# A Mamba-like two-layer network on one core: the hand-laid tables of interleavings are replaced

## The chip, the cores and the metric

The kernel runs on one core of one Trainium2 chip, in a single launch. The metric is device microseconds of that core, the median of three runs. The core has TensorE (PE in the profile, its weight loads PEld), VectorE (DVE), ScalarE (ACT), GpSimd (POOL) and SyncE (SP), which issues all DMAs of this kernel.

## The reference: what is computed

Eight samples go one after the other through two layers. Layer 0 is an input projection of 192 channels to 2 x 384, a depthwise 3x3 convolution, a state-space scan with two orders of the 64x64 image (12 heads of 64 channels, 32 states), a gate, an output projection and an MLP. Layer 1 has a branch of three dense convolutions and a branch with layernorm, projection, depthwise convolution and a selective scan in four directions over 192 channels with 16 states each:

```
def step(h, t):
    u_t, d_t, b_t, c_t = t
    h = jnp.exp(d_t[..., None] * A) * h + (d_t * u_t)[..., None] * b_t[:, :, None, :]
    return (h, jnp.einsum('bkdn,bkn->bkd', h, c_t))
```

The four directions are summed, normed, gated, projected, and joined with the convolution branch.

## The kernel before

**Slots.** The selective scan of layer 1 is the backbone. For one sample it is 384 units (4 directions x 4 column blocks x 24 groups of 8 channels x 16 states, a tile of 128 x 1024). A unit is handled in a slot. In slot u, ScalarE makes the decay `dA` of unit u+1 (exp, line 1202) from a 512 KB DMA `dA<-dld`; TensorE expands the input of unit u+1 into `PU` (2 matmuls, waits for scan u-1) and sums the product of unit u-3 into `PY` (4 matmuls); VectorE multiplies `PU` by B (line 1588) and runs the scan `H` (line 1820); GpSimd multiplies `H` by C into `HC` (line 1984). The scans are the same for every sample and follow one another without a break.

**Rounds.** Everything else is laid between the slots as steps. Round r (r = 1 to 8) holds the 384 scan slots of sample r-1, phases a to f of sample r, which prepare the next sample's scan, and, from round 2 on, the closing phases g and h of sample r-2. Round 0 has no scan. Round 1 is of kind "first", rounds 2 to 7 are "middle", round 8 is "last".

**Phases.** a: projection and depthwise convolution of layer 0 (`a.conv`), then tokens written to DRAM (`tkd`). b: the state-space part of layer 0 in chunks, 8 set-up steps (`b.setup`) and 64 units, each with `b.fetch` (SP loads `TK` from `tkd`), `b.prepare` (TensorE, ScalarE, GpSimd), `b.mix` (GpSimd, line 1917), `b.out` (TensorE, VectorE) and `b.store`. c: gate, output projection and MLP, 8 strips. d: three convolutions. e: layernorm, projection, depthwise convolution. f: the inputs of the scan (`f.steps`, `f.split`). g and h: sum of directions, norm, gate, output.

**What sets the order.** Each engine has its own table: for every third of a slot (`p` = 0, 1, 2) a digit says how many steps of the list are placed ahead of it. A step that has nothing to do on an engine costs nothing there. Where a middle round also holds phases g and h, a second table `AMID` says how their steps go between those of a to f. No scheduler acts at run time: each engine takes its instructions in the order written and waits on semaphores. The steps of a phase stand in the same order on every engine before and after; only where they fall among the slots differs.

```
    for slot, n in zip(slots, TAKEN.get((kind, engine), [0] * len(slots))):
        out += itertools.islice(left, n)
        out.append(slot)
    return out + list(left)
```

Of the kernel before, what the change touches and what calls it, by code (L numbers as in the profile page):

```python
# [174 lines left out]
def counts(text):  # L175
    out, n = [], 0
    for c in text:
        n += DIGITS.index(c)
        if c != "Z":
            out.append(n)  # L180
            n = 0
    return out
# [4 lines left out]
        "a0009000000003003002007400000002402000000000000000000000000000000000j00006000600000600000000006000000006000006"  # L187
        "00000000T00100100w00100010w00100100w00100100w00100100w00100010w00100100900000600100100100000000000500020100000"
        "40040040000050090050034020050045000050090053040034020050090077007050030013020050090050043020050090053061013020"
        "05007003402005007003402005004302005009005205003402005009503402000500304207005304003402005009007700705003001302"  # L190
        "00500900500330200400500000000000000000800010000300000330000000400100c00500000000400100100100200000400200500100"
        "00030020010020010000040020050010000050000010020010000040020050010000030030000020010001030020050010000030020010"
        "0200100000400300300100200100100100100000300300210000000200010200100000300000100000000000000000000b003003004003"
        "00300200400300500300300400300300300400300300300400300500300300400300300300400300300500300300400300300400400300"
        "30040030030050030030030040030030020000000050020020030010050030030020010000000000060020040040010020030040020010"
        "0400100200300200590000700800500900900900900900900900d00900900900500000000000000000000000b100002002004300004007"
        "4000020032030002007000002003030020020032020000023002"),
    ("first", "ACT"): counts(
        "c0000001000009000000a00000001000700000008003001000004000300000001000500000000001b00001001004001001000004600000"
        "00200220000100300Qx00001001000x0000100l000d0000l00000cx00001001000x00001001000e0000100000110000000200230000000"  # L200
        "0000900000004002c00002005007200007005002c00002005007700002007007j00002000005700002007007700005002007c020000050"
        "07200005007007200005007007200005007002c00002005007700002007007c00000002007c00002005007700002007007j00002000005"
        "700002007007700004002003006000000002002002000000000005000003200004000003e0000000000400000000400100000200400150"
        "00040000000000040010005000010010050040000000005000000000025000000050040000000000041000000020041000050040000000"
        "00004001000002004001400000003000300000000002300000000002400000002002100000000000000000006000100001001000100001"
        "001000m00000000000a0000000000b00000000b00000000b000000b00000000000b0000000000b00000000b00000000b000000b0000000"
        "0000b0000000000b00000000b00100000000c0002000000010024000010050033000030030011000000020035000010010044000000040"
        "01600001000007a00008009009900000009009i0000000100hi0000000100h00000000a001000000000001501001000002600003004003"
        "3000020030032000030050012000000080008000000010028000"),
    ("first", "DVE"): counts(  # L210
        "0e09000000007000003000000008600000200000000007001000000000000300000000000000000000O000000000000000000000000000"
        "00000000000Q00000000y00000000y00000000y00000000y00000000y00000000y00000000600000000000000900000201000202000000"
        "000000000a0070030430400340030430040070030430430400340030430430430430470030040070030430430040030430430430430040"
        "03043040034003043040034003043004007003043043040034003043043043004007003043043043040034003043043043043047003004"
        "00700304304003300303401000200000000000003102100003000000300102100004001b00500000000401000100200100002003002000"
        "00500100300100100210000200300200500000130100100000200100200300200000500100320000000200100200300200000500100300"
        "10010020010020030020000040030000010002000000000000009000002000000000000007000000010000020000000000000000000000"
        "00000000000000000000000000000000000000000000000000000000000000000000000000000000000000000000000000000000000000"
        "00000000000000000000000000000000000000000ZZZ200100200200300300300300300300000000000500200500500500000500000500"
        "000500000000000000900000680090000900900900900900900900900900900900900900300000000000000000000000000000000i00a0"  # L220
        "0300000600300700300000000600300700300000000000600300700"),
    ("first", "POOL"): counts(
        "000g0000040060000000090000080000000070040000040010000000000010000000000000000000000000000000000000000000000000"
        "0000000000Zy00000000y00000000y00000000y00000000y00000000y00000000y00000000000000000000000000000m00000000000000"
        "a00000700700000700700700000700700700000700700700700000700700700e0070000070070000070070070000070070070070070000"
        "0700700700000700700700000700700700000700700700700000700700700700700000700700700700700000700700700e007000007007"
        "00000700700600000600400000300000000000000200000000900000000000000b00000000000h00000000000000000000000000000000"
        "l00000000000000000000000000000000l00000000000000000000000000000000l00000000000000000000000000000000l0000000000"
        "0000000000000000000000000000000000000000000000000000000000000000000000000000000000000K000000000000000000000000"
        "00000000000000000000000000000000000000000000000000000000000000000000000000000000000000000000000000000000000000"  # L230
        "000000000000000000000000000000000000000ZZZ30000000000000000000000000000000000000000000000000000000000000000000"
        "0000000000000000000000Ze00800i00900000900r00000000900r00000000900900000000b00000000000000000000000000000000v00"
        "200000400300300400300200400000300300200200300400200300000"),
    ("first", "SP"): counts(
        "0000c000000006004000003600000004002000006002006000004004000002000000003000006006000006000000000006000006000000"
        "00600000000400R000002v0000200000x00100100w00100100w000002v0000200000x00100100d00100100100100000000400000400900"
        "00000060000000070070070070000070070000070070070070070000070070070077007000070000070070070070000070070070070070"
        "00007007007000007007007000007007000007007007007007000007007007007000007007007007007007000007007007007700700007"
        "00000700700100600000600700200000000000000000800000000000000000a00000000000g00000000000000000000000f00000600000"
        "000000000000000000000f00000600000000000000000000000000f00000600000000000000000000000000f0000060000000000000000"  # L240
        "0000000000f00000000000000000000000000000g000000000000000000b00000000000000000000007002001001000001001001000002"
        "00000000000000000000000000G00000000000000000000m00000000000000000m00000000000000000000m00000000000000000m00000"
        "000000000000m00000000000c00000000000c00500000000200300300300300300000000000000000000000c0000050000050000050000"
        "0500500000000500040000000000000000000000000000000000000000000000000000000ZZn0000000000000011000060020003000000"
        "0b00230000400600000300300300000a0000000060000030000064"),
    ("middle", "PE"): counts(
        "0t00000000400300300000200000300400200400200200000000000000000000000000000000g300006000000006000000006000006000"
        "000600600000T00100100w00100100w00100001w0010010000w00100100w00100100w00100100900000060000200000100000000000500"
        "02010000040040040050034020050030060052070053040020050070034020050070034020050043020050090052050034020050090077"
        "00705003001302005009007700705003001302005009005003402005009005003006005207005304003402005009007700705003001302"  # L250
# [2223 lines left out]
```

How the kernel before makes its waits and increments, by code:

```python
    def take_over(self, e, phase):  # L553
        for name, n in ENDS[phase]:
            e.wait_ge(*self.at(name, n, phase))
        for name in END_DMAS[phase]:
            of = (SHARED[name] if name in SHARED else DMAS[name])[phase]
            e.wait_ge(*self.at(name, of, phase))
# [269 lines left out]
def begin(e, X):  # L829
    if X.n == 0:
        e.wait_ge(X.K.S["b_dve"], SETUP["b_dve"])
    else:
        X.K.samples[X.n - 1].take_over(e, "f")
# [9 lines left out]
    def bank(step, j=0):  # L844
        held = X.before(step, j)
        if held:
            pe.wait_ge(*held)
        return X.bank(step, j)
# [4 lines left out]
    def a_turn(i, p):  # L854
        if p:
            return
        if X.n == 0 and i == 0:
            pe.wait_ge(S["b_dve"], SETUP["b_dve"])
        pe.wait_ge(*X.at(f"xin{i % 2}", 16 * (i // 2 + 1), "a"))
        for hh in range(2):
            pb = bank(("a.turn", i, 0), hh)
            for q in range(4):
                t = pe.transpose(pb[0:96, q * 128:(q + 1) * 128], K.XI[:, i % 2, q, hh * 96:(hh + 1) * 96], K.IDENT)
            t.then_inc(S["a_turn"], 1)
# [1 line left out]
    def a_project(i, j):  # L866
        if i == 0 and j == 0:
            pe.wait_ge(*X.at("weights", 32, "a"))
        pe.wait_ge(*X.at("a_xT", 2 * i + 2))
        pb = bank(("a.project", i, j))
        for k in range(2):
            t = mm(pb[:, :], K.wx[:, k, j * 128:(j + 1) * 128], K.XT[:, i % 2, k, :], k == 0, k == 1)
        t.then_inc(S["a_proj"], 1)
# [126 lines left out]
    def c_outp(i, m):  # L1000
        pe.wait_ge(*X.at("c_yr", 2 * (3 * i + 2) + 2))
        pb = bank(("c.outp", i, m))
```

## Time and profile before

| | us |
|---|---|
| median of 3 runs (18377.16 to 18397.39) | 18393.42 |
| the profiled execution, its own time | 18391.18 |
| its span, first to last instruction | 18389.4 |
| rounds 2 to 7 (13207.0), mean of one | 2201.2 |
| mean granted TensorE clock | 0.82 |

The profile gives busy time of an engine as a union of its instructions. In a stretch where two engines are busy for nearly all of it, both limit it; where none is, instructions wait for one another or for DMAs. A granted clock of 1.00 is 2.4 GHz, 0.50 is 1.2 GHz, and a value between is a mean over the stretch. Round r's scans stand in the trace at rows 384(r-1) to 384r of line 1820, so a slot has a time: round 4 runs from 7846.9 to 10051.4 us, and its slots 60, 79, 156, 162, 240, 250, 266, 305, 320 and 362 begin at 8232.2, 8337.3, 8827.6, 8861.2, 9230.8, 9270.6, 9377.4, 9578.7, 9658.8 and 9872.9 us. In phase b, slots 88, 100, 120 and 132 begin at 8387.0, 8452.1, 8590.9 and 8667.2 us. Round 1 runs from 1373.3 to 3437.8 us.

### The profile page before, as it was taken

To read this page: it belongs to the slowest core of one execution; us is meant where nothing else is said; L and a number is where in the kernel's file an instruction comes from. 1 tells how busy PE (TensorE), PEld (TensorE's weight loads), DVE (VectorE), ACT (ScalarE), POOL (GpSimd) and SP (SyncE) were. 2 spreads that over 40 slices of the span, in tenths; PEclk is the share of its full clock that TensorE was granted. 3 is DMA by queue.
4 is the path that set the end of the run, shared out by engine and by line. 5 is a ranking of instruction groups with operands and counts; after the bars stand their busy time and mean duration, and the time that the engine had idled before them with its cause. 6 is when DMAs were issued, how large, how long until landed. Compare 5 with 4: busy or idle time off the path is not lost. (4 is left out here: it accounts for less than half of the span.)

```text
span 18389.4 us, 229305 instructions
## 1 busy us (share of the span) xinstructions
PE 14799.7 (80%) x75328; PEld 6584.1 (36%) x75328; DVE 14337.4 (78%) x10683; ACT 9054.4 (49%) x15627; POOL 10798.0 (59%) x5940
## 2 busy tenths in 40 slices
PE   7877889788887888878888788878889788885655
PEld 5423533244332443235332353324523244331202
DVE  3237689877887788877888768887789777889997
ACT  3245445654456444664447544465445644455332
POOL 3225756756557665666557565575655766557563
PEclk8988898788888888887988889778798888886555
DMA  2226576756766578665786657765686666868775
GB/s 91 83 80 188 161 195 174 206 161 179 195 173 202 160 190 196 170 196 157 194 197 185 175 159 203 188 198 162 170 201 175 203 164 180 195 174 216 183 189 141
DMA packets 1564886, 3223.74 MB, mean 175 GB/s; under 512 B 296592, under 2 KB 730064, under 8 KB 1562192
## 3 DMA queue, kind: packets, MB, share of 16 engines
q1 hardware_dynamic: 1563728, 3209.07, 65.2%
q8 instruction: 632, 10.35, 0.3%
q14 instruction: 526, 4.31, 0.1%
HBM read 2474.94 MB, written 733.48 MB: 174 GB/s over the span
## 5 line engine op out<-in xcount | busy, mean ns | idle before, releaser
L1984 POOL TENSOR_TENSOR HC<-H,BR 128x1024 f32<-128x1024 f32 x3072 | 7357.2, 2399 | 4784.3 <-DVE H L1820 3268.2
L1820 DVE TENSOR_TENSOR_SCAN H<-dA,CR,PU 128x1024 f32<-128x1024 f32 x2304 | 5397.6, 2343 | 393.5 <-ACT CR L1202 212.6
L1202 ACT ACTIVATE dA<-dA,A 128x1024 f32<-128x1024 f32 x3072 | 3502.7, 1142 | 1607.4 <-DMA dA<-dld 1557.8
L1588 DVE TENSOR_TENSOR PU<-PU,BR 128x1024 f32<-128x1024 f32 x3072 | 3725.5, 1213 | 379.2 <-PE PU L852 345.9
L852 PE MATMUL PU<-PT,SELB 96*128 96x512 bf16 x6144 | 2282.1, 460 | 2022.8 <-DVE H L1820 1880.1
L852 PE MATMUL PB<-RA,RB 128*128 128x64 f32 (+3 forms) x10992 | 3128.6, 438 | 73.5 <-DVE RA L1591 68.0
L852 PE MATMUL PY<-HC,CB 128*32 128x256 f32 x24576 | 2409.4, 471 | 119.0 <-POOL HC L1984 108.5
L852 PEld LDWEIGHTS PB<-RA,RB 128*128 128x128 f32 (+2 forms) x10992 | 1745.1, 205 | 1357.8 <-issue 1240.5
L852 PE MATMUL PB<-RA 128*32 128x64 f32 (+2 forms) x11712 | 1723.2, 325 | 456.3 <-DMA RA<-tkd 392.9
L852 PEld LDWEIGHTS PU<-PT,SELB 96*128 96x128 bf16 x6144 | 545.4, 106 | 3685.4 <-issue 3484.8
L1820 DVE TENSOR_TENSOR_SCAN H<-dA,PU 128x1024 f32<-128x1024 f32 x768 | 1752.1, 2281 | 134.2 <-POOL HC L1984 70.4
L1917 POOL TENSOR_TENSOR RB<-RA,RB 128x768 f32<-128x768 f32 x512 | 930.4, 1817 | 1157.2 <-issue 647.4
L852 PEld LDWEIGHTS PB<-RA 128*32 128x32 f32 (+2 forms) x11712 | 1035.8, 164 | 1215.3 <-issue 564.9
L1202 ACT ACTIVATE RA<-PB 32x128 f32<-32x128 f32 (+3 forms) x2776 | 1078.4, 389 | 653.1 <-PE PB L852 608.3
L852 PE MATMUL PB<-RA,PX 96*128 96x512 f32 x2304 | 1131.8, 631 | 108.4 <-ACT RA L1202 95.1
L1202 ACT ACTIVATE YS<-PY 128x256 f32<-128x256 f32 x768 | 292.3, 381 | 1846.7 <-PE PY L852 1846.5
L852 PEld LDWEIGHTS PY<-HC,CB 128*32 128x32 f32 x24576 | 530.3, 119 | 1797.8 <-issue 1531.5
L1202 ACT ACTIVATE RB<-PB 128x128 f32<-128x128 f32 (+4 forms) x1344 | 364.5, 313 | 1442.7 <-PE PB L938 918.3
L1588 DVE TENSOR_TENSOR RA<-RA,PB 128x384 f32<-128x384 f32 x512 | 281.9, 551 | 944.4 <-PE PB L852 942.4
L1202 ACT ACTIVATE CR<-H 128x1 f32<-128x1 f32 x3072 | 590.9, 192 | 854.8 <-DVE H L1820 851.9
L852 PE MATMUL PB<-XT,RB 96*128 96x512 f32 x1536 | 794.9, 657 | 76.8 <-DMA XT<-xTd 39.7
L852 PE MATMUL PB<-RB 96*128 96x128 bf16 (+1 forms) x4608 | 640.4, 263 | 113.5 <-ACT RA L1202 94.7
(180 smaller groups left out, 17582.9 us busy)
## 6 DMA issues: line engine op xcount, KB each, us to landing
dA<-dld SPq DMA_DIRECT2D x3072, 512.0 KB, 6.0
PT<-ptd SPq DMA_DIRECT2D x2304, 64.0 KB, 4.3
BR<-bcd SPq DMA_DIRECT2D x256, 512.0 KB, 7.6
ptd<-RA SPq DMA_DIRECT2D x176, 576.0 KB, 5.8
y0d<-RA SPq DMA_DIRECT2D x512, 192.0 KB, 9.6
RA<-y0d SPq DMA_DIRECT2D x128, 768.0 KB, 6.7
yd<-YS SPq DMA_DIRECT2D x768, 128.0 KB, 5.0
tkd<-RB SPq DMA_DIRECT2D x256, 262.0 KB, 3.8
```

The source lines that it names most:

```text
L852: return nc.tensor.matmul(out, w, x, start=start, stop=stop, skip_group_check=True)
L1202: return ac.activation(out, in_, f, **kw)
L1588: return v.tensor_tensor(out, a, b, op)
L1820: v.tensor_tensor_scan(h, a, x, 0.0 if first else K.CR[:, gi:gi + 1], MUL, ADD).then_inc(S["s_scan"], 1)
L1917: po.tensor_tensor(K.MM[u % 2].rearrange("p (h t) -> p h t", h=6), K.EE[u % 2].rearrange("p (h t) -> p h t", h=6), K.GS[u % 2].unsqueeze(1 ...
L1984: po.tensor_tensor(K.HC[:, w % NHC, :], K.H[:, w % NH, :], K.BR[:, (w // 24) % NBR, 1, :], MUL).then_inc(S["s_mulC"], 1)
```

## The change

Only numbers in the tables `TAKEN` (all three kinds) and `AMID` (kind "middle") differ. No instruction is added, removed or resized; the same steps stand at other slots. This is the core of the diff, one line of two tables:

```diff
     ("middle", "PE"): counts(
-        "02010000040040040050034020050030060052070053040020050070034020050070034020050043020050090052050034020050090077"
+        "00044050060014030040021060071040030061042050034021042050034021042050034021042050034021042050034021042050034021"
...
 AMID = {
     ("middle", "PE"): counts(
-        "000000000000ZZZZZZZZZZZZZZZZV0000200000001m0000000n10000030000000l10000040000000o10000040000000l1000033000000b"
+        "000000000000ZZZZZZZZZZZZZZZZV0000600000003s0000000k00000110000000m10000010000000k10000020000000j0000002000000c"
```

Read out of the tables, the slots between which a phase of a middle round stands on VectorE (for d, the slots between `d.begin` and `e.begin`, in which g and h stand too):

| phase, middle round | slots before | slots after |
|---|---|---|
| b.setup, up to the first b.out | 69 to 79 | 67 to 76 |
| b, units | 79 to 156 | 76 to 160 |
| c | 157 to 250 | 161 to 257 |
| d with g, h | 250 to 317 | 257 to 320 |
| e | 317 to 362 | 320 to 360 |
| f (goes on in the next round) | 362 to 384 | 360 to 384 |

In round 1, b ends at 160 in place of 154, c at 261 in place of 249, e begins at 324 in place of 307 and ends at 357 in place of 353. In round 8 only the steps of g and h of sample 6 move, from slots 55 to 127 to slots 55 to 135.

**Place 1: TensorE in phase b of round 4, about slot 109.** `PU` and `PY` are the scan's own products; all rows with `PB` are steps of phase b. Before:

```order
L852 MATMUL PB<-NEGB,IDB 128x384
L852 MATMUL PB<-RA,RB 128x64 x6
L852 MATMUL PB<-RB 128x128 x3
L852 MATMUL PB<-NEGB,IDB 128x384
L852 MATMUL PB<-RA 32x64 x6
L852 MATMUL PB<-RA 128x128 x4
L852 MATMUL PB<-CB,RA 32x128 x3
L938 MATMUL PB<-CB,RA 32x128
L852 MATMUL PB<-RB 128x128 x3
L852 MATMUL PB<-NEGB,IDB 128x384
L852 MATMUL PU<-PT,SELB 128x512 x2
L852 MATMUL PY<-HC,CB 32x256 x4
```

After, at about slot 109 too:

```order
L852 MATMUL PU<-PT,SELB 128x512 x2
L852 MATMUL PY<-HC,CB 32x256 x4
L852 MATMUL PB<-RA 128x128
L852 MATMUL PB<-CB,RA 32x128 x3
L938 MATMUL PB<-CB,RA 32x128
L852 MATMUL PB<-RB 128x128 x3
L852 MATMUL PB<-NEGB,IDB 128x384
L852 MATMUL PB<-RA,RB 128x64 x6
L852 MATMUL PU<-PT,SELB 128x512 x2
L852 MATMUL PB<-RB 128x128 x3
L852 MATMUL PB<-NEGB,IDB 128x384
L852 MATMUL PB<-RA 32x64 x6
```

Before, two units stand between one pair of scan products and the next, and elsewhere none begins in a slot or two. After, the steps are cut finer: units begin 1.00, 1.33 and 1.67 slots apart in turn, over and over (before 0 to 2 slots apart, and 16 of 64 have their `b.fetch` on SyncE less than two slots ahead of their `b.prepare` on TensorE; after 2 of 64).

**Place 2: SyncE at the start of phase b, round 4.** `spd` and `RB` are small tables of b, `RA<-tkd` the first units' tokens, `BR` the scan's B and C. Before:

```order
L2025 DMA spd<-RA 128x3x128 x6
L2025 DMA dA<-dld 128x1x1024
L2025 DMA RB<-spd 3x1536 x2
L2025 DMA RA<-tkd 128x524
L2025 DMA RA<-tkd 128x1x454
L2025 DMA RB<-spd 3x1536 x2
L2025 DMA RA<-tkd 128x524
L2025 DMA RA<-tkd 128x1x454
L2025 DMA dA<-dld 128x1x1024
L2025 DMA yd<-YS 128x256
L2025 DMA BR<-bcd 128x1x1024 x2
L2025 DMA dA<-dld 128x1x1024
```

After:

```order
L2025 DMA spd<-RA 128x3x128 x6
L2025 DMA dA<-dld 128x1x1024
L2025 DMA PT<-ptd 32x1024 x3
L2025 DMA RB<-spd 3x1536 x2
L2025 DMA RA<-tkd 128x524
L2025 DMA RA<-tkd 128x1x454
L2025 DMA RB<-spd 3x1536 x2
L2025 DMA RA<-tkd 128x524
L2025 DMA RA<-tkd 128x1x454
L2025 DMA dA<-dld 128x1x1024 x3
L2025 DMA RB<-spd 3x1536 x2
L2025 DMA RA<-tkd 128x524
```

The `BR` loads stood right behind the first units' loads and one `dA`; now three `dA` and a third unit stand between them. The load that the first units wait for stands two slots earlier, and the first `b.prepare` on ScalarE behind it 1.3 slots later, not 3.

**Place 3: TensorE at the end of phase c, round 4, about slot 246.** `96x512` and `128x512` are the MLP's products. Before:

```order
L852 MATMUL PB<-PX,RB 96x512 x6
L852 MATMUL PY<-HC,CB 32x256 x4
L852 MATMUL PU<-PT,SELB 128x512 x2
L852 MATMUL PY<-HC,CB 32x256 x4
L852 MATMUL PU<-PT,SELB 128x512 x2
L852 MATMUL PY<-HC,CB 32x256 x4
L852 MATMUL PB<-PX,RB 96x512 x6
L852 MATMUL PU<-PT,SELB 128x512 x2
L852 MATMUL PY<-HC,CB 32x256 x4
L852 MATMUL PU<-PT,SELB 128x512 x2
L852 MATMUL PY<-HC,CB 32x256 x4
```

After:

```order
L852 MATMUL PB<-RA,RB 96x512 x6
L852 MATMUL PU<-PT,SELB 128x512 x2
L852 MATMUL PY<-HC,CB 32x256 x4
L852 MATMUL PU<-PT,SELB 128x512 x2
L852 MATMUL PY<-HC,CB 32x256 x4
L852 MATMUL PB<-RA,RB 128x512 x2
L852 MATMUL PU<-PT,SELB 128x512 x2
L852 MATMUL PY<-HC,CB 32x256 x4
L852 MATMUL PB<-RA,RB 96x512 x6
L852 MATMUL PU<-PT,SELB 128x512 x2
L852 MATMUL PY<-HC,CB 32x256 x4
L852 MATMUL PU<-PT,SELB 128x512 x2
L852 MATMUL PB<-RA,RB 128x512 x2
```

Before, nothing but scan products is left on TensorE from about slot 250 on until phase d; after, the MLP goes on to slot 259, in every slot or second slot.

## Rows read from the trace of the kernel before

**Rows 1.** Page of the profiled execution: its span.
```profile
span 18389.4 us, 229305 instructions
```

**Rows 2.** Windows, rounds 1 and 2 to 7: length; PE, PEld, DVE, ACT, POOL busy; clock, DMA.
```profile
1373.30:3437.80 2064.50, 1728.09 (x9030) 761.01 (x9030) 1698.60 (x1230) 1093.37 (x1898) 1315.45 (x731) 0.86 0.67 182
3437.80:16644.80 13207.00, 10981.67 (x56659) 4946.11 (x56659) 10677.99 (x7914) 6825.11 (x11760) 8100.57 (x4452) 0.84 0.68 183
```

**Rows 3.** Timeline of VectorE, two bare slots of round 8: start, length, instruction.
```profile
17318.64 2.35 DVE L1820 TENSOR_TENSOR_SCAN H<-dA,CR,PU 128x1024 f32<-128x1024 f32 x1
17320.90 1.21 DVE L1588 TENSOR_TENSOR PU<-PU,BR 128x1024 f32<-128x1024 f32 x1
17322.20 2.35 DVE L1820 TENSOR_TENSOR_SCAN H<-dA,CR,PU 128x1024 f32<-128x1024 f32 x1
```

**Rows 4.** Timeline of TensorE in one slot of round 4, full clock.
```profile
9004.59 0.59 PE L852 MATMUL PU<-PT,SELB 96*128 96x512 bf16 x2
9005.11 0.64 PE L852 MATMUL PY<-HC,CB 128*32 128x256 f32 x8
9005.68 0.67 PE L852 MATMUL PB<-PX,RB 128*96 128x512 f32 x1
```

**Rows 5.** Windows of round 4, stage by stage (columns as in rows 2).
```profile
8232.20:8337.30 105.10, 56.97 (x335) 24.19 (x333) 86.18 (x68) 44.06 (x90) 49.60 (x25) 0.68 0.70 167
8337.30:8827.60 490.30, 422.84 (x3725) 287.26 (x3724) 341.24 (x344) 220.48 (x546) 342.89 (x265) 0.83 0.57 159
...
8861.20:9230.80 369.60, 341.30 (x1392) 125.53 (x1392) 343.12 (x252) 178.32 (x264) 205.82 (x85) 0.96 0.75 197
9230.80:9270.60 39.80, 30.15 (x132) 9.35 (x128) 36.55 (x27) 18.46 (x26) 23.73 (x11) 0.85 0.78 204
9270.60:9377.40 106.80, 71.33 (x242) 20.28 (x242) 77.31 (x50) 35.49 (x56) 61.45 (x26) 0.64 1.04 210
9377.40:9578.70 201.30, 198.10 (x881) 88.98 (x880) 192.10 (x143) 90.49 (x147) 90.48 (x38) 1.00 0.79 201
9578.70:9658.80 80.10, 62.50 (x287) 32.39 (x289) 66.64 (x44) 26.39 (x47) 43.20 (x34) 0.53 0.66 171
9658.80:9872.90 214.10, 192.37 (x702) 60.34 (x694) 199.77 (x131) 151.19 (x207) 122.08 (x59) 0.88 0.55 145
9872.90:10051.40 178.50, 131.61 (x377) 41.32 (x378) 140.35 (x66) 131.61 (x179) 146.27 (x58) 0.76 0.68 207
```

**Rows 6.** Windows in phase b of round 4, all engines.
```profile
8387.00:8452.10 65.10, 56.08 (x524) 37.93 (x523) 51.63 (x51) 29.22 (x72) 48.42 (x36) 0.88 0.59 165
8452.10:8827.60 375.50, 320.63 (x2767) 217.69 (x2767) 249.66 (x254) 163.93 (x408) 254.25 (x197) 0.81 0.57 157
8590.90:8667.20 76.30, 65.44 (x558) 43.39 (x558) 52.32 (x52) 31.78 (x79) 51.95 (x40) 0.80 0.58 160
```

**Rows 7.** The same three windows, scans alone (line 1820).
```profile
8387.00:8452.10 65.10, 27.86 (x12) 0.88 0.59 165
8452.10:8827.60 375.50, 129.85 (x56) 0.81 0.57 157
8590.90:8667.20 76.30, 28.11 (x13) 0.80 0.58 160
```

**Rows 8.** The same three windows, GpSimd's b.mix alone (line 1917), one a unit.
```profile
8387.00:8452.10 65.10, 14.52 (x8) 0.88 0.59 165
8452.10:8827.60 375.50, 85.49 (x47) 0.81 0.57 157
8590.90:8667.20 76.30, 16.36 (x9) 0.80 0.58 160
```

**Rows 9.** Waits in phase b, 8452.1 to 8827.6: us, times, longest us.
```profile
DVE RA L1588 <- PE PB L852: 123.9, 64, 7.2
...
ACT dA L1202 <- DMA dA<-dld: 64.5, 18, 5.9
...
PE PB L852 <- DMA RA<-tkd: 43.4, 25, 3.2
```

**Rows 10.** Waits of ScalarE, 8302 to 8337.3: us, times, longest us.
```profile
ACT dA L1202 <- DMA dA<-dld: 15.0, 1, 15.0
```

More of the change, by code:

```diff
@@ new lines @@
+        "0042008000029026054002020031072020020000000000000000"),
+    ("first", "ACT"): counts(
+        "c0000001000009000000a00000001000700000008003001000004000300000001000500000000001h00000000000600000000001500000"
+        "001001X00001001000x0000100l000d0000l00000cx00001001000w00001001000x00001001000e0000100000110000000200230000000"
+        "0000900000000006c00002000007c00002005002c00002005002c00002005002c00002005002c00002005002c00002005002c000020050"
+        "02c00002005002c00002005002c00002005002c00002005002c00002005002c00002005002c00002005002c00002005002c00002005002"
+        "c00002005002c00002005002c00002005002900000000006000004000002000000005003600000000002f0000000000040000000400100"
+        "000200000a000000004000000000000004100000002000a000000000040000000000005000000020005050000000040000000000005000"
+        "00000002500000005004000000000000500000000002500000004003000000000003000000004001200002000000200000000002300000"
+        "000000000000006000200000001001200000000001b00000000000a00000000000a00000000000b00000000000b00000000000b0000000"
+        "0000b0000000000a10000000000ba00001000000b0000000000a10000000000b00000b000000b00001000000c00000002000h000020000"
+        "07100000002007t0000100r00i00000000000A000000000000r0900000000000000i00000000000000a001000000000000101003003002"
+        "k00007002006d0000b00000070000100a0010000050000000000"),
@@ new lines @@
+        "0000000000000000l000000000000000000000000000000000000000000000000000000000000000000000000000000000000000000000"
+        "00000000000K00000000000000000000000000000000000000000000000000000000000000000000000000000000000000000000000000"
+        "000000000000000000000000000000000000000000000000000000000000000000000000000000000000000000000ZZZ30000000000000"
+        "0000000000000000000000000Z600p00i00000000A00000000000000r00900000000000i00000000000000b00000000000000000000000"
+        "000H00000b00800400300400200300500200500200000000000000000"),
@@ new lines @@
+    ("first", "SP"): counts(
+        "0000c000000006004000003600000004002000006002006000004004000002000000003000006006000600000006000000000006000000"
+        "006000004Q0000200000x00010100w00100100w000002v00002000001v0000200000x00010100d00100100100100000000400000000400"
+        "90000006000070000077000070000070070070000070070070000070070070000070070070000070070070000070070070000070070070"
+        "00007007007000007007007000007007007000007007007000007007007000007007007000007007007000007007007000007007007000"
+        "00700700700000700700700000700100600000a00300200000000000000800000000000000a000000000000g0000000000000000000000"
+        "f000000006000000000000000000000000000f00000000006000000000000000000000000f00000000006000000000000000000000000f"
+        "00000000006000000000000000000000000f0000000000000000000000000000000000g000000000000000000000000b00000000000000"
+        "00000000700300000100100000200000110000000000000000000000000000000000000000000000G00000000000000000000000m00000"
+        "000000000000000m00000000000000000m00000000000000000m000000000000000000m0000000000c00000000c005000002003c000000"
+        "0000000000000m00f50000400000000000000000000000000000000000000000000000000000000000000ZZn0000000000000008020000"
+        "0300b50000a0040096040020030060070010050000060000000000"),
@@ new lines @@
+    ("middle", "PE"): counts(
+        "0t000000002005003000002000000007002004002002000000000000000000000000000000g00300006000000006000006000006000600"
+        "000006000002R00100100w00100100w00100001w0010010000w00100100w00100100w00100100900060100110000000000500020100000"
+        "00044050060014030040021060071040030061042050034021042050034021042050034021042050034021042050034021042050034021"
+        "04205003402104205003402104205003402104205003402104205003402104205003402104205003402104205003402104205003402104"
+        "205003402104205003402104205003302103203000000000000000000009003000004300300001000g0100000000600000100200000100"
+        "30030050000050000010000020010000010030030050000060000010020001000030030050000030010020000020010001000030030040"
+        "01001002003000001002000100003003003001003001000100001000001003002002001000001001000100003000003000001000000000"
+        "00000000j00000000000200200200500000400200e00300300b00300200300600i00200300300200600100c00d00300300100200500m00"
+        "200300500500300k00400200100100600l00100500d1001005080060010010000081000000000000040020020050030030030010040010"
+        "00000008004001004001001003004500005005107305009009009009009009009009009009009009009009000000000000000000000006"
+        "e006082020050050056033043042002013020070022000000000"),
@@ new lines @@
+    ("middle", "ACT"): counts(
+        "0000o001200001006001003006000000101000007000500003001002100000003001400000000000500000001005600000001003800000"
+        "001001a00000000002T0000l00000az00001001000x0000100l000c0000100000ld0000l00000ce0000200000050000000000230000000"
+        "0000900000000006c00002000007c00002005002c00002005002c00002005002c00002005002c00002005002c00002005002c000020050"
+        "02c00002005002c00002005002c00002005002c00002005002c00002005002c00002005002c00002005002c00002005002c00002005002"
+        "c00002005002c00002005002c00002005002900000000006000004000002000000005003600000000003e0000000000040000400100020"
+        "00000050050040000000000000040010002000000050050040000000005000000000025000000090000000000000041000000000025000"
+        "00005004000000000004100000000002500000004003000000000003000000004001200000002000200000000002300000000000000000"
+        "00600020000000000200000000000210100300l00020000000d00c00000000b003j0000000000c000003003000j0000000b00130000300"
+        "j000b01003000003j0000000c00030000300i00160000h00200330000f0010014000000050013000000000014000000050033000010050"
+        "04100000004003401003002003504000000000s09009009000909009009000909009009000909000000000a01000000000000000000002"
+        "e0000e00800100000000b0088030000000076030030000005000"),
@@ new lines @@
+        "0000l00000000000000000000000000000000000000000000000000000000000000000000000000000000000000000000000000000000K"
+        "00000000000500000000000000300000000000000000000000000000000000000000000000000000000000000000000000000000000000"
+        "000000000000000000000000000000000000000000000000000000000000000000000000000000ZZZZZ100000000000000000000000000"
+        "000000000000000000000000000000000000000000000000Zv00900900000i00i00000000i00i00000000i00000000000b000000000000"
+        "00000000000x00a00900400300700300600000300700300400000000000"),
@@ new lines @@
+    ("middle", "SP"): counts(
+        "06003003000004006000000003001005000004002000000600002003002001004004002000000003000006000000006000006000006000"
+        "00600000600000400000R10000100w001w00001001001w0000100100w00010000x00100100w000002d0000100100220000200000000400"
+        "90000006000070000077000070000070070070000070070070000070070070000070070070000070070070000070070070000070070070"
+        "00007007007000007007007000007007007000007007007000007007007000007007007000007007007000007007007000007007007000"
+        "00700700700000700700700000700100600000a00300200000000000000800000000000000a000000000000g0000000000000000000f00"
+        "000600000000000000000000000000000f000006000000000000000000000f00000006000000000000000000000000000f000000000060"
+        "00000000000000000000000f0000000000000000000000000000000000g000000000000000000000000b00000000000000000000007004"
+        "00000000200000900000300000000300000000000400000000500H00000000000800o00000000000000500000w00000000000000500w00"
+        "000000000000500w00000000000000500z00000100800g00000100600g0000050000000000050012020000020030030030030030000000"
+        "0000000000c00000500000000500050000500000590000000000000000000000000000000000000000000000000000ZZn0000002000000"
+        "00000b0000700900a00300c00400400500000a0030010050000060"),
```

204 lines of the change are left out of this document (69 added, 135 removed).

## The prediction

> **What bounds the kernel now.** I read the page first, then windows cut at the rounds, then windows cut at the slots where the phases of round 4 change, then the waits inside the longest phase, and last the timelines that give the price of a slot. The page gives a span of 18389.4 us [rows 1]. The six middle rounds take 13207.0 us of it, 2201.2 each, and in them TensorE is busy for 83% (10981.67), VectorE for 81% (10677.99), at a granted clock of 0.84 [rows 2]. Neither engine is full, so the loss must be in stretches where one of them waits, and where the work falls among the slots can matter.
>
> The smallest slot is VectorE's own: a scan and a product begin 3.56 us after the last pair (17322.20 - 17318.64) [rows 3]. TensorE's part of a slot is small: its two groups of products take 1.09 us at full clock (9005.68 - 9004.59) [rows 4]. So 384 bare slots would be 1367 us of 2201, and the rest is side work.
>
> The stages of round 4 [rows 5] show four kinds of stretch. Set-up of b, slots 60 to 79: 105.1 us with TensorE at 56.97 and VectorE at 86.18, one stall among them, of 15.0 us, in which ScalarE waits for a `dA` transfer [rows 10]. Phase b: 490.3 us for 77 slots, TensorE 422.84, VectorE 341.24, clock 0.83. Phase c: 369.6 us for 78 slots, both engines at 92%, clock 0.96. Around d: slots 250 to 266 take 106.8 us with TensorE at 71.33 and clock 0.64, slots 266 to 305 are full (TensorE 198.10 of 201.3, clock 1.00), slots 305 to 320 take 80.1 us at clock 0.53. So there is lull, full, lull. Phase e: VectorE 199.77 of 214.1.
>
> Inside b the same work runs at two rates. Slots 88 to 100 take 65.1 us, 5.43 a slot, at 0.88; slots 100 to 156 take 375.5 us, 6.71 a slot, at 0.81 [rows 6] (12 and 56 scans [rows 7]). The first holds 8 units and the second 47, by GpSimd's `b.mix` [rows 8]: 0.67 and 0.84 a slot. Per unit that is 8.1 and 8.0 us, the same. In the second stretch VectorE waits 123.9 us for TensorE's b products, and TensorE waits 43.4 us in 25 waits for tokens (`RA<-tkd`) [rows 9].
>
> **The change part by part**, for a middle round. Nothing is added or removed, so the sum is of slots that a phase gains or loses, and of waits that go.
>
> *Set-up of b:* between slot 60 and b's first output stand 16 slots where there were 19. The 3 slots go over to other phases: -3 x 3.56 = -10.7. Of moved steps SyncE's count too: the `BR` loads now stand three `dA` and one unit later, so the `dA` queued behind the first units' loads come earlier, but the first `b.prepare` on ScalarE follows its load after 1.3 slots, not 3, and ScalarE's next `dA`, thus VectorE's scan, stands behind it. I leave the 15.0 us [rows 10] as it is: bounds -15 (gone) and +6 (1.7 slots of lead lost, at 3.56 each, if nothing covers it).
>
> *Phase b:* 84 slots in place of 77, 0.76 units a slot. The stretch at 0.67 units cost 5.43 a slot, the one at 0.84 cost 6.71 [rows 6, 8]. The line through both gives 5.43 + (0.76 - 0.67) x 1.28 / 0.17 = 6.1; but the second is uneven (0 to 2 slots between units) and waits 43.4 us for tokens that are fetched under two slots ahead, 16 times in 64. After, that happens twice. If those waits go, 0.77 us a slot goes (43.4 / 56), at least where they bind; I take half, and 5.7 a slot: 84 x 5.7 = 479, against 490, so -11. Bounds: 84 x 5.43 = 456 (-34), and 84 x 6.36 = 534 (+44), the rate of slots 120 to 132 (76.3 / 12) [rows 6], the uneven pattern with few units (9 [rows 8]). `b.mix` stands behind `HC` on GpSimd and `b.out` ahead of scans on VectorE; both have room (254.25 and 249.66 of 375.5 [rows 6]).
>
> *Phase c:* 157 to 250 becomes 161 to 257, 3 slots more. Where TensorE has no idle time a slot more costs 1.09 [rows 4], where VectorE has none 3.56 [rows 3]: +3 to +11, and I take +5, since both are at 92% [rows 5].
>
> *d with g and h:* 70 slots become 63, and the MLP's end now fills the lull ahead of d. Lower bound of the gain: 7 x 1.09 = 7.6. Upper: 7 x 3.56 = 24.9. In the lulls (250 to 266, 305 to 320) TensorE is idle for 53 of 187 us [rows 5], in between it has no room, so the true value lies between; I take -20, nearer to the upper end, since the full clock that the middle has may reach the edges.
>
> *Phase e:* 42 slots become 40: -2.2 to -7.1, I take -5, VectorE being at 93% [rows 5]. *Phase f:* 22 become 24, +2.2 to +7.1; with VectorE at 140.35 of 178.5 [rows 5] some of this has cover, but I take +5. Where these slots' products are hidden, VectorE hides them; if e or f is late, the next round's first scan is late.
>
> Sum of a middle round: -10.7 - 11 + 5 - 20 - 5 + 5 = -37; six are -222. Round 1 (2064.5 us [rows 2]): b and c in the same new form, -10 and +6; d has 63 slots in place of 58 (261 to 324, was 249 to 307), +12 (five slots, between 1.09 and 3.56 each); e comes into 33 slots from 46, where VectorE binds: at 1.09 to 3.56 a slot -14 to -46, I take -20, as its other work is now dense. Together -12. Round 8 moves only steps of g and h over 80 slots in place of 72; VectorE has the same instructions there, so 0. Total -234. The profiled execution's own time is 18391.18, 2.2 below the median: 18391 - 234 = 18157, **18160** in round numbers.
>
> The Trainium skill ("TensorE: Matmul & The Clock Gate", section "HAM oscillation — how this bites in real kernels") tells that a kernel with short bursts of matmuls between waits for DMAs is throttled again at every burst. The trace agrees in so far as b, with its 25 waits for tokens, has 0.81 and the dense stretch of d has 1.00 [rows 5, 9]; by that rule alone b after the change would be the rival below with the full clock.
>
> **The rivals.**
>
> *B keeps its time per unit.* What b does may be bound by a unit's chain through TensorE, ScalarE, GpSimd and back, and not by the spread: 8.1 us a unit at 0.67 a slot and 8.0 at 0.84 [rows 6, 8] speak for it. Then 64 units take 64 x 8.0 = 512 less what overlaps, in any pattern, so b stays at 490 or gains little, and the fewer slots elsewhere meet TensorE: at 1.09 each for d and e, -9.8; set-up -10.7; c and f +5.5; b +0 to +4. Per round -11 to -15, over all -70 to -90: 18,310. Against it: the 43.4 us of waits on tokens, which can go.
>
> *Slower: b costs by the slot.* Slots 120 to 132 hold 9 units like the new pattern (0.75) and cost 6.36 each [rows 6, 7, 8]. At that rate b takes 534 us in place of 490, +44; the other terms give -26; +18 a round, +108 in all: 18,500. It decides once a slot of b costs more than (490 + 26) / 84 = 6.14 us. For it: the line through both rates gives 6.1. Against: that stretch lies within the uneven pattern, and pays waits and the low clock of its neighbours.
>
> *Even work holds the clock.* In c, TensorE never rests for long and has 0.96; in d 1.00 [rows 5]. If b, with a unit begun every 1.33 slots, had 2.4 GHz too, its TensorE work of 422.84 at 0.83 would be 423 x 0.83 = 351, or 4.2 a slot, below VectorE's (341.24 + 7 x 3.56 = 366, 4.4), and the slot would be about 5.2, as in c (4.74) and more for the chain: 84 x 5.2 = 437, -53; -79 a round, -490 in all: 17,900. Against it: the even stretch 88 to 100 has only 0.88. The Trainium skill (the same page, "Part 4: PE-mode transpose") speaks against it as well: transposes don't count as busy there the same way. No run here shows that by itself.
>
> **How the numbers follow.** Forecast 0.50 (18,060 to 18,260); b keeps its time per unit 0.25 (about 18,250 to 18,370); slower 0.12 (above 18,420 mostly); full clock 0.13 (below 18,050). The range leaves out the slower case and part of the full clock: 18,000 to 18,390. A measurement tells no change within 0.2%, 37 us, so 18,356 to 18,430: that takes the upper end of the second case and the lower of the third. Faster 0.77, same 0.12, slower 0.11.
>
> **What would show it.** In round 4 of the changed kernel: b's 84 slots in about 479 us (at 450 the clock rival, at 510 or more the slower), its clock at or above 0.88, TensorE's waits for `RA<-tkd` down from 43.4 us to under 15; the 15.0 us wait for `dA` still there; slots 257 to 320 in about 368 us (slots 250 to 320 took 388.2 [rows 5]); clock of d's edges above 0.7. It would be wrong if b's waits are merely renamed, so that VectorE's wait for TensorE stays at 124 us, or if the dense e of round 1 waits on its own chain.

## The result: 18442.82 us, 0.35% slower

The changed kernel takes 18442.82 us (median of 7 runs, 18423.58 to 18478.92), the kernel before 18377.16 (7 runs, 18370.89 to 18409.07): ratio 1.0035, 95% interval 1.0025 to 1.0045. Forecast were 18160 and a range of 18000 to 18390, so the direction was wrong. The profiled execution has a span of 18421.8 us, 32.4 more than before [rows 1]:

```profile
span 18421.8 us, 229276 instructions
```

Windows of the changed kernel, round 1 and rounds 2 to 7 (columns as in [rows 2], which they answer to):

```profile
1371.80:3457.30 2085.50, 1723.42 (x9027) 760.12 (x9028) 1701.81 (x1230) 1079.26 (x1886) 1316.96 (x730) 0.86 0.66 180
3457.30:16683.20 13225.90, 10942.95 (x56663) 4938.85 (x56662) 10575.25 (x7914) 6781.36 (x11751) 8076.56 (x4453) 0.86 0.68 183
```

Round 1 is 21.0 us longer (2085.5, was 2064.5), the six middle rounds 18.9 together (13225.9, was 13207.0). So it isn't that nothing changed: gains and losses of some 20 us in each round cancel. Round 4 of the changed kernel, cut where its phases now stand (set-up; b; c; d with g and h; e; f):

```profile
8243.00:8331.70 88.70, 49.06 (x314) 22.01 (x312) 78.32 (x64) 38.53 (x78) 40.32 (x20) 0.73 0.69 165
8331.70:8842.20 510.50, 428.03 (x3783) 288.72 (x3783) 363.77 (x358) 227.96 (x567) 363.14 (x273) 0.83 0.60 164
...
9303.20:9677.20 374.00, 323.37 (x1336) 140.25 (x1336) 308.95 (x218) 143.52 (x233) 176.65 (x90) 0.83 0.82 196
9677.20:9893.10 215.90, 196.09 (x686) 61.81 (x686) 176.10 (x129) 143.50 (x199) 115.43 (x57) 0.86 0.50 135
9893.10:10076.80 183.70, 135.76 (x398) 42.96 (x398) 149.72 (x69) 136.64 (x188) 149.11 (x60) 0.79 0.69 208
```

Against [rows 5]: b takes 510.5 us in 84 slots, at the same clock (0.83) and with nearly the same TensorE time (428.03, was 422.84) as in 77. The mean over rounds 2 to 7, from the starts of the scans in both traces, is steadier than one round (from round to round a stage varies by 1 to 3 us, d by 6):

| stage of a middle round | before | after | difference | forecast |
|---|---|---|---|---|
| slots 0 to 60 | 383.4 | 381.6 | -1.8 | 0 |
| to b's start | 105.0 | 89.2 | -15.8 | -10.7 |
| b | 490.2 | 509.9 | +19.7 | -11 |
| end of b to the first gate (6 slots) | 33.5 | 37.3 | +3.8 | 0 |
| c, gate to end | 410.0 | 424.4 | +14.4 | +5 |
| d with g and h | 387.3 | 366.9 | -20.4 | -20 |
| e | 214.0 | 212.3 | -1.8 | -5 |
| f | 177.7 | 182.5 | +4.9 | +5 |
| round | 2201.2 | 2204.3 | +3.1 | -37 |

Set-up, d and f came near their forecasts. Of the 40 us a round that are missing, 31 are in b and 9 in c. Waits in b of round 4, changed kernel (us, times, longest), all engines and then SyncE's queue:

```profile
ACT dA L1202 <- DMA dA<-dld: 165.2, 41, 6.4
DVE RA L1588 <- PE PB L852: 137.9, 79, 6.5
...
PE PB L852 <- DMA RA<-tkd: 63.1, 38, 4.7
```

```profile
SPq L2025 <- PE PB L852: 94.4, 32, 5.3
```

The same two waits in b of round 4 of the kernel before:

```profile
PE PB L852 <- DMA RA<-tkd: 49.8, 30, 3.2
```

```profile
SPq L2025 <- PE PB L852: 91.3, 32, 6.0
```

The waits for tokens, which the even pattern was to remove, are still there: 63.1 us over all of b, where they were 49.8. ScalarE's waits for `dA` are long (165.2, were 75.6), and SyncE waits 94.4 us for TensorE, once for every second unit, as it did before (91.3). These were the three suspects, and the first experiments took them in turn.

### The profile page after: what moved, and what is told of

Its sections match the earlier page's. It is cut to its first block and busy times, and to the rows that moved or that the text cites. A ratio compares the mean times of both kernels' runs of the same rounds, so it can differ in the third digit from the quotient of the medians.

```text
span 18421.8 us, 229276 instructions
## 1 busy us (share of the span) xinstructions
PE 14765.0 (80%) x75328; PEld 6583.6 (36%) x75328; DVE 14228.4 (77%) x10683; ACT 8997.5 (49%) x15605; POOL 10774.0 (58%) x5940
## 5 line engine op out<-in xcount | busy, mean ns | idle before, releaser
L852 PE MATMUL PB<-T,RA 128*128 128x512 f32 (+1 forms) x1024 | 617.4, 731 | 152.3 <-ACT B L1202 40.6
```

What stands on the lines that cost most here:

```text
L852: return nc.tensor.matmul(out, w, x, start=start, stop=stop, skip_group_check=True)
```

## The experiments

Ratios are to the kernel before, run beside it on the same chip. Where a rule moves steps, it works on the third of a slot (`at`) ahead of which the tables put each step, in rounds 1 to 7.

**e1: the lump in phase c.** In the changed kernel, all gate steps of strip 2 stand ahead of one slot.

```diff
+SPREAD = {"PE": [520] * 6 + [523] * 2 + [526] * 2 + [529] * 2, "ACT": [521] * 6 + [529] * 3 + [532] * 3,
+          "DVE": [523] * 5 + [525] * 2 + [528] * 2 + [529] * 2 + [532]}
+        if to and X.n == r and ((name, i) == ("c.gate", 2) or (name, i) == ("c.mlp", 0) and p):
+            new[m] = to.pop(0)
```

> The changed kernel, with the gate steps of strip 2 and the MLP steps of strip 0 beside them spread over slots 173 to 177 on TensorE, ScalarE and VectorE (rounds 1 to 7), where the new tables have them all ahead of one slot. In the changed kernel slot 174 of a middle round takes 20.4 us. Theory A (the lump leaves TensorE and VectorE taking turns with no scan to cover them): slots 166 to 180 lose 8 to 12 us a round, 55 to 85 us over seven rounds, and the kernel comes level with the one before (18377) or just below it. Theory B (phase c costs by its work, however cut): 0 to 3 us a round, the time stays at 18420 to 18443.

18417.84 us, ratio 1.0042 (1.0026 to 1.0058). Slots 166 to 180 take 88.1 us in the mean middle round, 86.9 in the changed kernel. Theory B, as far as the edit reaches: slot 174 falls from 20.4 to 15.5 us, and the three slots behind it take 5.9 more. What stays of the lump isn't tested.

**e2: b at its old slots.** The tables `TAKEN` of kinds "first" and "middle" are replaced: all steps stand as in the changed kernel, but for the units of b, which stand as before. The first line of one table:

```diff
+TAKEN["middle", "PE"] = counts(
+    "0t000000002005003000000002000000007002004002002000000000000000000000000000000g00300006000000006000006000006000600"
...
```

> The changed kernel with the units of phase b at their old slots (79 to 156 on VectorE, uneven) in rounds 1 to 7; all other steps as changed, so slots 76 to 79 and 156 to 160 are bare. Theory A (b pays by its work, and a slot more in it costs less than a bare one, 19.7 / 7 = 2.8 against 3.56 us): slots 76 to 160 take 490 + 7 x 3.56 = 515 us in a middle round, 5 more than the 509.9 of the changed kernel, the kernel 30 to 40 us slower than the changed one. Theory B (the even pattern is itself bad for b): 505 us or less, the kernel 30 us faster or more.

18502.31 us, ratio 1.0076 (1.0060 to 1.0093). Slots 76 to 160 take 526.2 us in the mean middle round, 16 more than the 509.9 of the changed kernel. So 7 slots inside b cost less (19.7) than bare ones around it (7 x 3.56 = 25), as A says, and the even pattern isn't what harms b. The excess over A's 515 lies ahead of b: slots 76 to 79, bare in e2, take 24.1 us and not 10.7, while b itself takes 487.6.

**e3 and e4: the order in the queues.** Each `b.fetch` behind its slot's `dA` load on SyncE (e3); b's steps one slot earlier on ScalarE (e4).

```diff
+    return [n + (X.n == r and name == "b.fetch") for n, (X, (name, i, p)) in zip(at, side)]
...
+    return [max(n - 3, first) if o else n for n, o in zip(at, own)]
```

> The changed kernel with each b.fetch on SyncE one third of a slot later, just behind the dA load of its slot and not ahead of it. In the changed kernel SyncE waits 94 us in phase b of round 4 for TensorE to free a token buffer, with a dA load queued behind, and ScalarE waits 165.2 us for dA (75.6 before the change). Theory A (this queue is what makes b slow): ScalarE's waits fall to under 110 us, phase b by 10 to 25 us a round, 70 to 170 us in all. Theory B (ScalarE is ahead of need there, its waits cost nothing): the waits fall and the time stays within 15 us; or the tokens come later and b gets 5 us a round slower.

> The changed kernel with all steps of phase b one slot earlier on ScalarE alone, so that they stand ahead of a dA exponential that they stood behind. Theory A (b's ScalarE steps come late because they stand behind a dA that has not landed): b falls by 10 to 25 us a round, 70 to 170 us in all. Theory B (ScalarE's place does not bind): within 15 us. If the steps now wait for TensorE with dA behind them, scans come late and b gets slower by 5 us a round or more.

18444.15 us (1.0049, 1.0034 to 1.0064) and 18422.07 us (1.0038, 1.0023 to 1.0053). In round 4 of both, ScalarE's waits for `dA` are no longer among the seven longest in b, where they led with 165.2 us, and waits for TensorE have taken their place; b takes 514.7 and 508.8 us in round 4 (510.5), 514.5 and 511.4 in the mean (509.9). Theory B, twice, in e3 by its second branch: the tokens come later (TensorE waits 72.7 us for them) and b is 4.6 us slower. ScalarE is busy for 228 of the 510 us, so its waits could change their name and leave the length of b as it was; neither place in a queue is what bounds b.

**e5, e6, e8: a third buffer for b's small tables.** `b.fetch` of an even unit waits for an `RL` buffer; with three it waits for unit u-5, not u-3. e5 has it on the changed kernel, e6 on the kernel before, e8 as e5 with the fetches two thirds of a slot earlier.

```diff
-            if u >= 3:
-                sp.wait_ge(*X.at("b_decay", 2 * (u - 3) + 2))
+            if u >= 6:
+                sp.wait_ge(*X.at("b_decay", 2 * (u - 5) + 2))
...
-                dma(K.RL[c % 2][32 * w:32 * w + 3, w, :],
+                dma(K.RL[c % 3][32 * w:32 * w + 3, w, :],
```

> The changed kernel with a third buffer RL for phase b's small tables of decays (RB<-spd), so that b.fetch of an even unit waits on SyncE for the decay products of unit u-5 in place of u-3. In the changed kernel SyncE waits 94.4 us in 32 waits, one for every second unit, for TensorE in b of round 4, with the tokens' loads behind, and TensorE is idle for 82 us of 510, 63.1 of them in waits for the tokens. Theory A (the second RL buffer comes free too late, so the tokens are fetched late wherever the tables put the fetch): SyncE's waits for TensorE fall under 40 us, TensorE's for tokens to under 35, b by 25 to 50 us a round, 170 to 350 us in all: 18090 to 18270. Theory B (the tokens' transfer itself is slow, or the five token buffers bind as well): within 5 us a round, and some 3 us more in set-up for the added memsets.

> The kernel before, with the same third RL buffer. In its b of round 4, SyncE waits 91.3 us in 32 waits for TensorE and TensorE 49.8 us for tokens. Theory A: b falls by 15 to 40 us a round from 490, the kernel to 18100 to 18260, and the changed tables are then worth what was predicted of them or not: by the forecast the changed kernel with three RL is faster than this by 150 us or more, by the price of slots that the traces show (2.8 us a slot in b) the two are within 60 us. Theory B: no change beyond the memsets' 3 us a round.

> The changed kernel with three RL buffers and each b.fetch from the fifth on two thirds of a slot earlier on SyncE. Theory A (with the buffer free the fetch can go early, and tokens then land in time): TensorE's waits for tokens fall under 15 us in b of round 4 and b is another 5 to 15 us a round faster than with three RL alone. Theory B (the five token buffers bind next): SyncE waits again for TensorE with dA loads behind, no gain over three RL alone.

18504.25 us (1.0068, 1.0044 to 1.0092), 18385.52 us (1.0014, 1.0005 to 1.0024), 18474.43 us (1.0064, 1.0047 to 1.0081). Theory A falls. SyncE's waits for TensorE stay (98.5 us in 32 in e5), and so do those for tokens:

```profile
PE PB L852 <- DMA RA<-tkd: 61.5, 34, 4.5
```

One reason to wait was taken away and the wait is as long as before; what it waits for then isn't told by these runs. Set-up, which has the memsets for the third RL, takes 4 us more a round in e5 (slots 60 to 76: 93.0 for 89.2) and 3 in e6. The mean middle round of e5 is 14 us longer than that of the changed kernel; the other 10 are spread over b, c and d and stay unexplained.

**e7: short dA loads.** One load of 512 KB a slot is cut to an eighth; seven eighths of the decays' input is left out.

```diff
-        dma(K.dA[:, u % NA, :],
+        n = 1024 if u < NA else 128
+        dma(K.dA[:, u % NA, 0:n],
```

> The changed kernel with each dA load cut to 128 of its 1024 columns (after the first five), so seven eighths of the decays' input is left out; TensorE, VectorE, ScalarE and GpSimd do the same instructions. Theory A (the tokens wait because SyncE issues them late): TensorE still waits 40 us or more for tokens in b of round 4 and b takes 480 us or more. Theory B (the tokens' transfers are slowed by the dA transfers beside them, and ScalarE's 165 us of waits for dA delay b): the waits go, b falls to 450 us or less, a few hundred us in all.

17380.38 us, ratio 0.9468 (0.9445 to 0.9491). Round 4, b (columns as in [rows 2]):

```profile
7856.50:8236.00 379.50, 363.87 (x3783) 246.41 (x3783) 356.77 (x357) 225.84 (x561) 360.77 (x273) 0.97 0.38 118
```

131 us of b are gone, with the same instructions on every engine, and little elsewhere: the mean middle round falls from 2204.3 to 2050.6 us, 130 of the 154 in b; slots 180 to 257 take 336.8 us (337.6), slots 320 to 384 395.2 (394.8). The rest of the 154 is mostly in d with g and h (355.2 for 366.9), slots 0 to 60 (374.8 for 381.6) and set-up (84.5 for 89.2). So transfers bind b, and b far more than any other stage, though its mean DMA share was only 0.60. Theory B holds, but whether through bytes, buffers or something else is not told by it: the share says that bytes aren't short. Three windows of the changed kernel, 2, 3 and 4 us long, around the token load of an odd unit:

```profile
8598.00:8600.00 2.00, 2.00 (x17) 1.40 (x18) 1.91 (x1) 0.07 (x1) 2.00 (x1) 0.87 1.04 259
8601.00:8604.00 3.00, 3.00 (x19) 1.80 (x18) 1.52 (x2) 1.62 (x7) 2.54 (x3) 0.50 0.13 47
8605.00:8609.00 4.00, 4.00 (x34) 2.81 (x34) 2.58 (x3) 1.28 (x5) 2.33 (x2) 0.83 0.91 246
```

The share (before last) falls from 1.04 to 0.13, which is 2 of 16 engines, and back to 0.91. Of the 70 packets that the trace has in the middle window, 59 are of 1816 bytes (the column load of an odd unit) and 8 of 4096 (a `dA` load's). Over all of b, a column load's 128 packets take 7.9 us from first to last in the mean (5.4 to 9.7). Counted microsecond by microsecond, the share is under 0.2 in 160 of the 510 us of b; packets of 1816 and 1536 bytes (the store of an odd unit) are 60% of the packet time in them, and 27% is that of 4096 bytes. It was so before the change too: 166 of 490 us.

The reason is in the form of these two DMAs: `tkc[c]` and `ycol[c]` are two columns (w) of 64 pixels, first dimension 2. The Trainium skill ("DMA: Bandwidth & Descriptors", section "Why a DMA increments its semaphore by 16 and not by 1") says that a DMA is spread over the largest number of engines, at most 16, that divides the slowest dimension of both sides; for these that is 2, and the trace agrees with its 0.13.

**e9, e10, e11: the transfers split.** The load (e9), and load and store (e10; e11 on the kernel before), as two DMAs of 64 rows.

```diff
-            dma(K.TK[u % 5][:, 0:454], tkc[c][:, :, 70:524], f"tki{u % 5}")
+            for w in range(2):
+                dma(K.TK[u % 5][64 * w:64 * w + 64, 0:454], tkc[c][w][:, 70:524], f"tki{u % 5}")
...
+        if k:
+            for w in range(2):
+                dma(ycol[c][w], K.YO[u % 4][64 * w:64 * w + 64, :], f"yo{u % 4}")
```

> The changed kernel with the token load of each odd unit of b (128 rows of 1816 bytes, a column of the image) issued as two DMAs of 64 rows, one for each column, in place of one. In the trace of the changed kernel the DMA share stands at 0.13, two engines of 16, for 5 to 8 us at each such load, and at the 1536-byte store of each odd unit. Theory A (these run on two engines alone, whose queues also hold an eighth of every dA, so b is bound by those two: 32 x (64 x 94 + 64 x 71 ns) = 338 us, and 84 slots x about 2.1 us of dA, PT and BR = 176, sum 514 us against 510 measured): loads of 64 rows spread over 16 engines, and b of round 4 falls by 32 x 5 = 160 us at most, to where TensorE binds: 380 to 420 us; 18442 - 7 x 100 = 17700 or so. Theory B (the tokens wait on buffers or on bytes per second): b stays at 500 us or more, or is slower by the added issues on SyncE.

> As e9, with the store of each odd unit split into two DMAs of 64 rows as well. Theory A: the share of 0.13 is gone from b, TensorE's waits for tokens under 10 us, its clock above 0.93, b of round 4 at 375 to 395 us (379.5 with short dA loads), the kernel at 17500 to 17650. Theory B: as e9.

> The kernel before with both splits. Theory A: b of round 4 from 490 to 370 to 385 us in its 77 slots, the kernel near 17530. Against e10 it tells what the tables are worth once the two DMA engines no longer bind b: by the trace prices with TensorE as the bound (+8 for b, +14 c, -16 set-up, -20 d a round) e10 is 60 to 150 us faster than this; by the zero sum of slots found so far they are within 40 us.

17501.99 us (0.9527, 0.9514 to 0.9540), 17326.04 us (0.9430, 0.9415 to 0.9444) and 17220.03 us (0.9375, 0.9362 to 0.9387). Phase b of round 4 in e9, in e10, and in e11 (77 slots):

```profile
7893.70:8278.80 385.10, 368.50 (x3780) 248.97 (x3779) 357.02 (x357) 225.67 (x559) 359.88 (x273) 0.95 0.79 218
```

```profile
7799.10:8160.00 360.90, 354.40 (x3779) 240.34 (x3779) 356.43 (x358) 224.27 (x558) 358.97 (x273) 1.00 0.86 231
```

```profile
7781.70:8133.10 351.40, 345.94 (x3717) 237.08 (x3716) 336.00 (x344) 218.84 (x546) 342.52 (x266) 0.99 0.84 226
```

Theory A. The same bytes and the same instructions, but for the added issues: b from 510.5 to 360.9 us in e10, DMA share from 0.60 to 0.86, TensorE, VectorE and GpSimd busy for 98 to 99% and the granted clock at 1.00, its upper level. A column load's 128 packets take 2.2 us from first to last, not 7.9. The longest waits of e10 in b are these, and TensorE has none for tokens; microseconds with a share under 0.2 are 6 of 360:

```profile
ACT RB L1202 <- PE PB L938: 62.9, 38, 2.3
PEld PB L852 <- issue: 45.1, 142, 1.9
ACT RA L1202 <- PE PB L852: 34.8, 23, 1.9
```

Theory A's sizes were too small: it had 375 to 395 us for b in e10, next to the 379.5 of e7, in which the odd units' transfers were still on two engines and the clock was 0.97, and 370 to 385 for e11. And e10 is 106 us slower than e11: the new tables cost 0.6% with the transfers unbound as well, where one expectation had a gain of 60 to 150 us and the other a tie within 40.

**e12: the other way.** In the kernel before, the row loads of even units are given first dimension 2 too.

```diff
-            dma(K.TK[u % 5], K.tkd[c * 128:(c + 1) * 128, :], f"tki{u % 5}")
+            dma(K.TK[u % 5], K.tkd[c * 128:(c + 1) * 128, :].rearrange("(h a) n -> a h n", a=2), f"tki{u % 5}")
```

> The kernel before, with the token load of each even unit of b, 128 rows of 2096 bytes in one block of memory, read as two interleaved halves of 64 rows (first dimension 2, as the column loads have it). The tokens of a chunk are permuted by it, so its results are other ones; sizes and instructions are the same. Theory A (a DMA whose first dimension is 2 is carried by two of the 16 engines, and these bind b): 64 x 124 ns more on the two, less the 8 x 124 that they carried, 6.9 us for each of 32 loads, b of a middle round from 490 to 700 to 715 us, the DMA share at 0.13 during these loads too, and the kernel near 20000. Theory B (the column loads are slow because their rows lie 64 rows apart in memory, and the first dimension is nothing): rows two apart are as quick as before, b within 20 us of 490.

19547.41 us, ratio 1.0651. Phase b of round 4 (77 slots):

```profile
8909.20:9537.50 628.30, 484.03 (x3720) 319.75 (x3719) 342.14 (x345) 220.90 (x545) 343.73 (x265) 0.71 0.43 124
```

And TensorE's waits for tokens in it:

```profile
PE PB L852 <- DMA RA<-tkd: 127.9, 38, 9.0
```

Rows that lie two apart in one block of memory slow b by 138 us, where A had 210 to 225 and B under 20. And e9 and e10 left the column rows 64 apart and were quick. It is the form of the DMA, not the distance of its rows. The size was too high in part because these packets are shorter than I took: 97 ns each in the trace, not 124, which makes 32 x (64 x 97 - 8 x 126) ns = 166 us.

## Why the prediction was wrong

**Phase b is the step that failed.** It said: "If those waits go, 0.77 us a slot goes (43.4 / 56), at least where they bind; I take half, and 5.7 a slot". The waits for tokens didn't go, they rose from 49.8 to 63.1 us in b of round 4, and a slot costs 6.07 us: b grew by 19.7 us a round where -11 was forecast. I had put the waits down to short leads (16 fetches under two slots ahead). The sign that I had named, VectorE's wait for TensorE staying where it was, came true as well: 145.6 us in b of round 4 before, 137.9 after. Shown by e7 and e9 to e12: they come from two DMA engines that carry the odd units' loads and stores alone, beside their part of every other transfer. An estimate from the trace's packets: 32 x (64 x 92 + 64 x 72) ns = 336 us a round, however the units are spaced, and what is left is (490.2 - 336) / 77 = 2.0 us a slot before and (509.9 - 336) / 84 = 2.1 after, close to the 8 packets of 243 ns that a `dA` load gives each engine (1.9 us). The fit is rougher than it looks: it takes loads and stores to be on the same two engines, which the packets don't name, and it leaves out the even units' transfers, `PT` and `BR`, some 80 us an engine. With them the packet times add up to about 590 us for the 510 of b, since packets overlap on an engine. The experiments carry the cause, not this sum. It fits what no rival of mine explained: 7 more slots for the same units cost 19.7 us, 2.8 each, and evenness brought nothing. The line through the two rates of [rows 6, 8], which I worked out (6.1) and then left for 5.7, was right: 84 x 6.1 = 512 for the measured 509.9.

**Phase c was mis-sized**: +14.4 for the +5 of "3 slots more". Its first gates take 79.4 us in 12 slots where they took 77.2 in 14, so two slots fewer saved nothing there, and the rest has 79 slots for 74, 345.1 for 332.8 us, 2.5 each. Counting slots from end to end hid five behind three. e1 gives no sign that the lump in it is the cause; why the dense start gains nothing is open.

**Right in size**: set-up (-15.8 for -10.7), d with g and h (-20.4 for -20), f (+4.9 for +5), and e nearly (-1.8 for -5). Two of these are partly luck. In set-up, ScalarE's 15.0 us wait for `dA` was to stay, and it is gone (its longest between slots 60 and 79 of round 4 is 4.0); the three slots that went over to b, 76 to 79, had taken 24.1 us, and the 16 that stayed grew from 80.9 to 89.2. In d, the clock of both edges was to be above 0.7: in round 4 slots 257 to 266 still have 0.65 and take 67.3 us, and only the rear edge, slots 305 to 320, rose from 0.53 to 0.83; the six rounds scatter by 6 us, so -20.4 is good to some 4. Round 1 was to gain 12 and lost 21.0; 17.3 of it are b (511.0 us in 84 slots for 493.7 in 78, 2.9 a slot), the same price as in the middle rounds, and c grew by 17.4 where +6 was forecast. Round 8 was to stay: its 384 scans gained 10.0 (1595.2 to 1585.2), the whole to the last instruction 5.6, and why is open.

**The rivals.** "Slower: b costs by the slot" had the direction and a point of decision at 6.14 us a slot. b came to 6.07, just short of it, and the 9 us of c and 4 us of the bubble behind b did the rest. "B keeps its time per unit" fails (7.66 to 7.97 us a unit). "Even work holds the clock" fails for the change: b has 0.83, even or not. With the transfers out of the way b has 1.00 and takes 361 us (e10), with a TensorE time of 354.40 for the 351 that the rival had worked out; but the uneven pattern has 0.99 too (e11), so it isn't evenness that gives the clock. The Trainium skill's remark on transposes, which I held against it ("TensorE: Matmul & The Clock Gate", "Part 4: PE-mode transpose"), did not speak for this kernel: b has one transpose (line 938, 0.28 us) in each unit, and 1.00.

**What the change is worth without the two engines**: e10 less e11 in a middle round is 2053.5 - 2040.7 = +12.8 us: b +13.2 (1.9 a slot), c +16, the bubble +5, f +5, against set-up -7, d -15, slots 0 to 60 -4. Slots only move from one phase to another; each costs 2 to 5 us where it is added, and one that is taken away saves 0.2 to 2.5.

## What to carry to other kernels

A mean DMA share of 0.6 is not an idle DMA system: cut the stretch into pieces of a few microseconds, and where the share stands at a few sixteenths (here 2), look for a DMA whose first dimension is that small. When the order of instructions is changed and waits change their names but the stretch keeps its length, the bound may be something that the order doesn't touch; e7, which shortened one kind of transfer, showed in one run that it was the transfers, and the trace in short windows then showed which. A table that gives slots to one phase takes them from another: sum what each slot costs and saves at both ends, phase part by phase part, before any gain from evenness.

## What the runs showed of the hardware

DMAs of 128 rows with first dimension 2 ran at a share of 0.13, and their loads' packets took 7.9 us from first to last; as two DMAs of 64 rows they take 2.2 us, at the price of one more issue on SyncE (about 0.5 us) each. The two engines delayed transfers that were spread over all 16 as well: a 512 KB `dA` load, whose 8 packets of 244 ns make about 2 us of each engine (an estimate), took 11.5 us from issue to landing in the median over b of the changed kernel, and 5.3 in e10. And the clock followed: 0.83 in b with 63 us of waits for tokens, 1.00 with none, on the same matmuls (TensorE's busy time 428.03, then 354.40 us).
